# Cross-attention and expert feed-forward on one core: keys and queries as two float32r terms in two row tiles instead of three bf16 terms in one

## What is computed

```python
x = x + xattn(layernorm(x), ctx, ctx)     # x: (2, 512, 256); ctx: (2, 1024, 256); 16 heads of 16
#   q, k, v = heads(Q W_Q' + b_Q), heads(K W_K' + b_K), heads(V W_V' + b_V)
#   scores = einsum('bhqd,bhkd->bhqk', q, k) / 4 ; probs = softmax(scores) ; attn = probs v
#   return attn W_O' + b_O
x = x + ffn(layernorm(x))                 # shared expert (512 hidden, silu gate)
#   plus 8 routed experts (256 hidden, gelu), the two best per token, gates from sigmoid scores
```

## Time and the profile before

| | |
|---|---|
| median of 3 runs | 416.05 us (414.91 to 416.39) |
| the profiled execution | 414.85 us, its span 412.9 us |
| PE busy, share of span | 384.8 us, 93% |
| DVE busy | 308.0 us, 75% |
| ACT busy | 206.6 us, 50% |
| POOL busy | 138.7 us, 34% |
| mean granted TensorE clock | 0.988 |

### The profile page before, as it was taken

The page is one execution under the profiler, slowest core; times in us unless marked ns, Lnnn a source line. Parts: engine busy times, 40 slices in busy tenths (PEclk is TensorE's granted clock), DMA queues, the critical chain, the costliest instruction groups (busy, mean ns, idle before and its releaser), DMA issues.

```text
span 412.9 us, 6040 instructions
## 1 busy us (share of the span) xinstructions
PE 384.8 (93%) x2208; PEld 215.3 (52%) x2208; DVE 308.0 (75%) x487; ACT 206.6 (50%) x373; POOL 138.7 (34%) x147
## 2 busy tenths in 40 slices
PE   6775979999999999999999899999999979999996
PEld 2562557222222222227222224348898878899995
DVE  4498967988888879884888862505777986686885
ACT  4653433877776776763777967662133131412111
POOL 2649997000403104040040220101038757007750
PEclk9998989999999999999999989999999999999999
DMA  7678438006151240610610100001013222102331
GB/s 244 232 162 188 118 86 223 0 2 116 53 115 54 57 104 10 115 54 2 116 52 2 52 2 1 3 1 54 0 41 88 76 78 84 46 2 58 96 102 51
DMA packets 23964, 30.34 MB, mean 73 GB/s; under 512 B 4672, under 2 KB 20992, under 8 KB 23168
## 3 DMA queue, kind: packets, MB, share of 16 engines
q1 hardware_dynamic: 23936, 29.98, 28.4%
HBM read 24.00 MB, written 5.77 MB: 72 GB/s over the span
## 4 chain that ended last, share of the span: by engine, by line
PE 76%; DVE 11%; DMA 4%; ACT 3%; issue 3%; POOL 2%; SPq 1%; ACTq 0%; DVEq 0%
PE psum L933 32%; PE psum L1052 14%; PE psum L1017 14%; PE psum L1027 12%; DVE negm L826 6%; PE psum L1061 2%; ACT PB L618 2%; DMA PB<-in_ctxT_dram 2%; DVE x_sb L814 2%; POOL R L497 1%; DMA QS<-qs_d 1%; DMA qs_d<-RAW 1%; PE psum L945 1%; DVE WH L796 1%; DVE WH L797 1%
## 5 line engine op out<-in xcount | busy, mean ns | idle before, releaser
L826 DVE TENSOR_REDUCE negm<-psum 128x1 f32<-128x1024 f32 x128 | 150.9, 1218 | 27.6 <-PE psum L1027 26.6
L618 ACT ACTIVATE PB<-psum 128x512 f32<-128x512 f32 x256 | 133.4, 604 | 56.4 <-PE psum L1017 56.1
L1017 PE MATMUL psum<-QS,KS 98*128 98x512 bf16 x256 | 81.1, 384 | 3.6 <-ACT PB L618 3.3
L1027 PE MATMUL psum<-KS,QS 96*128 96x512 bf16 x256 | 78.0, 389 | 5.9 <-DMA QS<-qs_d 3.7
L633 ACT ACTIVATE PB<-psum 128x512 f32<-128x512 f32 x40 | 22.1, 596 | 93.4 <-PE psum L933 93.4
L1052 PE MATMUL psum<-PB,VA 128*17 128x512 f32 x512 | 68.0, 605 | 0.0
L556 POOL TENSOR_SCALAR R<-RAW 128x512 fp32r<-128x512 f32 x32 | 23.2, 725 | 120.1 <-DMA RAW<-in_ew_dram 62.7
L1017 PEld LDWEIGHTS psum<-QS,KS 98*128 98x128 bf16 x256 | 20.0, 96 | 77.1 <-ACT PB L618 57.3
L933 PE MATMUL psum<-R,WH 128*128 128x256 f32 (+1 forms) x336 | 51.9, 302 | 3.8 <-POOL R L497 2.9
L933 PEld LDWEIGHTS psum<-R,WH 128*128 128x128 f32 x336 | 45.9, 191 | 7.9 <-issue 5.0
L933 PE MATMUL psum<-XT,R 128*128 128x512 f32 x192 | 46.7, 392 | 0.0
(11 more groups left out here) (128 smaller groups left out, 388.0 us busy)
## 6 DMA issues: line engine op xcount, KB each, us to landing
RAW<-in_ew_dram SPq DMA_DIRECT2D x32, 256.0 KB, 2.7
ks_d<-PARTS SPq DMA_DIRECT2D x16, 192.0 KB, 2.8
KS<-ks_d SPq DMA_DIRECT2D x8, 384.0 KB, 4.7
QS<-qs_d SPq DMA_DIRECT2D x48, 64.0 KB, 4.9
KS<-ks_d SPq DMA_DIRECT2D x8, 256.0 KB, 5.4
qs_d<-RAW SPq DMA_DIRECT2D x8, 192.0 KB, 3.2
RAW<-in_sw_dram SPq DMA_DIRECT2D x6, 256.0 KB, 2.9
x_sb<-in_x_dram SPq DMA_DIRECT2D x2, 512.0 KB, 6.1
```

What stands on the lines that cost most here:

```text
L618: act.activation(PB[:, n % PR, i * N:(i + 1) * N], bank[(2 * n + i) % 3], ACT.Exp, scale=DK ** -0.5).then_inc(exp_done, 1)
L826: dve.tensor_reduce(negm[:, g % 2, r // QT, r % QT:r % QT + 1], psum[:, k0:k0 + 2, :].rearrange("p a n -> p (a n)"), AX.X, ALU.max, negate ...
L1017: pe.matmul(bank[t % 3], KS[s][0:KROWS + 2, j, k0:k0 + P], QS[s][0:KROWS + 2, j, :], start=True, stop=True).then_inc(scores_done, 1)
L1027: last = pe.matmul(ring_bank(st, half), QS[s][0:KROWS, j, qt * P:(qt + 1) * P], KS[s][0:KROWS, j, half * N:(half + 1) * N], start=True, st ...
```

## The change

Keys and queries become two float32r terms (hi, lo). The stack of a group has 48 rows, the three products hi x hi, hi x lo, lo x hi, and two bias rows. It lies twice in the partitions: KS rows 0 to 49 hold the first 512 keys, rows 64 to 113 the other 512; QS holds the same queries in both halves. A score pair is now the same 128-key offset in either half (rows 0 to 49 and 64 to 113), so that its two matmuls use different row tiles of 64 rows, and so do the two matmuls of a maximum. Per K or Q job ACT writes the high term, DVE the low one straight from PSUM (one `scalar_tensor_tensor`), and POOL nothing; a ring of six part buffers takes the place of three. Stores and loads of the stacks move 4 bytes an element. The transpose of the maxima is in float32. `xn` has a buffer of its own, and `nrow` one slot.

```diff
-TERMS = 6
+TERMS = 3
+HP = P // 2
-POOL_MID = 6
+PARTS_RING = 6
-        QS = [sb(f"QS{i}", [P, GH, S], BF16) for i in range(SLOTS)]
-        KS = [sb(f"KS{i}", [P, GH, T], BF16) for i in range(SLOTS)]
+        QS = [sb(f"QS{i}", [P, GH, S], F32R) for i in range(SLOTS)]
+        KS = [sb(f"KS{i}", [P, GH, T // 2], F32R) for i in range(SLOTS)]
...
+            def store_parts(c):
+                kind, b, m, tb = kq_jobs[c]
+                n = jobs.index(kq_jobs[c])
+                sp.wait_ge(job_free[n % 4], n // 4 + 1)
...
+                    if kind == "K":
+                        sp.dma_start(dst[:, 0, :], half[:, 0, :]).then_inc(kq_stored[c][l], 16)
+                        sp.dma_start(dst[:, 1:3, :], half).then_inc(kq_stored[c][l], 16)
...
             def load_stack(g):
+                if g < SLOTS:
+                    sp.wait_ge(ones, g + 1)
+                for tb in range(2):
+                    sp.wait_ge(stored_k[tb][l], 32)
+                    sp.dma_start(raw(KS[s][tb * HP:tb * HP + KROWS, :, :]),
+                                 ks_d[b, m, l, :, :, :, tb * N:(tb + 1) * N].rearrange("p d j t -> (p d) j t"))\
                         .then_inc(stk_loaded[s], 16)
+                sp.wait_ge(stored_q[l], 32)
+                for tb in range(2):
+                    sp.dma_start(raw(QS[s][tb * HP:tb * HP + KROWS, :, :]),
+                                 qs_d[b, m, l].rearrange("p d j t -> (p d) j t")).then_inc(stk_loaded[s], 16)
...
                 for c in range(2):
-                    sp.dma_start(QS[g % SLOTS][KROWS + c:KROWS + c + 1, :, :],
-                                 nrow[GH * c:GH * c + GH, g % 2, :]).then_inc(bias_loaded[g % 2], 16)
+                    for tb in range(2):
+                        r = tb * HP + KROWS + c
+                        sp.dma_start(raw(QS[g % SLOTS][r:r + 1, :, :]), nrow[GH * c:GH * c + GH, :])\
+                            .then_inc(bias_loaded[g % 2], 16)
...
-                    act.activation(TMP[:, c % 3, :], bank[n % 4][:, :], ACT.Identity, bias=bias).then_inc(kq_hi, 1)
-                    act.activation(parts[c % 3][:, 0, :], bank[n % 4][:, :], ACT.Identity, bias=bias)\
-                        .then_inc(job_free[n % 4], 1)
+                    act.activation(parts[c % PARTS_RING][:, 0, :], bank[n % 4][:, :], ACT.Identity,
+                                   bias=kq_bias(kind, m)).then_inc(kq_hi, 1)
...
-                if kind in "KQ" and kq_of[jobs[n]] < POOL_MID:
+                if kind in "KQ":
-                    link(dve.tensor_tensor(TMP[:, c % 3, :], TMP[:, c % 3, :], parts[c % 3][:, 0, :], ALU.subtract))
-                    dve.tensor_copy(parts[c % 3][:, 1, :], TMP[:, c % 3, :]).then_inc(kq_mid, 1)
+                    dve.scalar_tensor_tensor(out=lo, in0=bank[n % 4][:, :], scalar=kq_bias(kind, m), in1=raw(hi),
+                                             op0=ALU.add, op1=ALU.subtract).then_inc(job_free[n % 4], 1)
...
-                        k0 = (2 * kp + i) * P
-                        pe.matmul(bank[t % 3], KS[s][0:KROWS + 2, j, k0:k0 + P], QS[s][0:KROWS + 2, j, :],
+                        rows = slice(i * HP, i * HP + KROWS + 2)
+                        pe.matmul(bank[t % 3], KS[s][rows, j, kp * P:(kp + 1) * P], QS[s][rows, j, :],
...
-                        last = pe.matmul(ring_bank(st, half), QS[s][0:KROWS, j, qt * P:(qt + 1) * P],
-                                         KS[s][0:KROWS, j, half * N:(half + 1) * N], start=True, stop=True)
+                        rows = slice(half * HP, half * HP + KROWS)
+                        last = pe.matmul(ring_bank(st, half), QS[s][rows, j, qt * P:(qt + 1) * P],
+                                         KS[s][rows, j, :], start=True, stop=True)
...
-                                         nhl[:, g % 2, qt].rearrange("p c j -> p (c j)"), identb[:, :],
+                                         raw(nhl[:, g % 2, qt].rearrange("p c j -> p (c j)")), ident[:, :],
```

More of the change, by code:

```diff
@@ L136, in xattn_ffn @@
     steps += [("mid", 3), ("split", 4), ("mid", 4), ("stats", 1), ("job", 5), ("rstd", 1), ("job", 6), ("mid", 5)]
-    steps += [("norm1", 1), ("ones", 0), ("job", 7), ("split", 5), ("mid", 6), ("split", 6), ("mid", 7), ("ones", 1)]
+    steps += [("norm1", 1), ("job", 7), ("split", 5), ("mid", 6), ("split", 6), ("mid", 7), ("ones", 1)]
     m = 0
@@ L391, in _ @@
               .then_inc(ld_rows, 16)
-            term_rows = [(3, slice(0, 3 * DK)), (2, slice(3 * DK, 5 * DK)), (1, slice(5 * DK, 6 * DK))]
+            def store_parts(c):
+                kind, b, m, tb = kq_jobs[c]
+                n = jobs.index(kq_jobs[c])
+                sp.wait_ge(job_free[n % 4], n // 4 + 1)
+                src = raw(parts[c % PARTS_RING])
+                for l in range(2):
+                    half = src[l * HP:(l + 1) * HP]
+                    if kind == "K":
+                        dst = ks_d[b, m, l, :, :, :, tb * N:(tb + 1) * N].rearrange("p d j t -> (d j) p t")
+                        sp.dma_start(dst[:, 0, :], half[:, 0, :]).then_inc(kq_stored[c][l], 16)
+                        sp.dma_start(dst[:, 1:3, :], half).then_inc(kq_stored[c][l], 16)
+                    else:
+                        dst = qs_d[b, m, l].rearrange("p d j t -> (d j) p t")
+                        sp.dma_start(dst[:, 0:2, :], half).then_inc(kq_stored[c][l], 16)
+                        sp.dma_start(dst[:, 2, :], half[:, 0, :]).then_inc(kq_stored[c][l], 16)
@@ L411, in load_stack @@
-                sp.wait_ge(stored_q, 32)
-                for n, rows in term_rows:
-                    for r0 in range(rows.start, rows.stop, DK):
-                        sp.dma_start(QS[s][r0:r0 + DK, :, :].rearrange("r j t -> r (j t)"),
-                                     qs_d[b, hg // 2, hg % 2, 3 - n].rearrange("d j t -> d (j t)"))\
-                            .then_inc(stk_loaded[s], 16)
+                m, l = hg // 2, hg % 2
+                stored_k, stored_q = kq_stored[kq_count(b, m):][:2], kq_stored[kq_count(b, m) + 2]
@@ L737, in route @@
                 ts = slice(4 * b, 4 * b + 4)
-                (lg, e_, s_, sel_, eq, w_, oh, oh2, both, prod) = (rt[:, i, ts] for i in range(10))
+                (lg, e_, s_, sel_, eq, w_, oh, oh2, both, prod) = (rt[b][:, i] for i in range(10))
                 dst = comb[:, ts, :]
@@ L1051, in _ @@
                     for j in range(GH):
-                        last = pe.matmul(acc[32 * j:32 * j + DK + 1, :], VA[:, b, 2 * kp + kk, GH * hg + j, :],
+                        last = pe.matmul(acc[32 * j:32 * j + DK + 1, :], VA[:, b, kp + KP * kk, GH * hg + j, :],
                                          PB[:, (4 * q + j) % PR, kk * N:(kk + 1) * N],
```

112 lines of the change are left out of this document (34 added, 78 removed).

## The result

The changed kernel takes 445.72 us (median of 4 runs, 443.3 to 446.53), the kernel before beside it 415.48 (413.83 to 416.39): the ratio is 1.0723, interval 1.0667 to 1.0779. It is 30 us slower. The forecast was 415.3, in a range from 402 to 427: the prediction is wrong.

The account below looks back on a forecast made before the run. The closed loop score, exponential, fourth score, maximum, pv was taken to bound the kernel. Terms -6.4, +4.2, 0, +2.0, -1.0, 0, +0.5 sum to -0.7: 414.15, plus 1.2 for the median, 415.3 us; range 402 to 427.

Parts of the forecast that it names:

- The clock falls in the waits: Rival: TensorE's waits let its granted clock fall; judged small, as a period is still 87% busy; chance 0.02.
- The period: Two units in the loop: 2.75 us instead of 2.88, 49 periods, -6.4 us (-9.8 to -2.9).
- The reading of the loop: Score, exponential, fourth score, maximum, pv form a closed loop; the fourth score waits for ACT's first exponential, until 1.13 us.
- A float32r weight load adds some 0.02: Up to a period's fourth score: the load moves the end of the wait for ACT from 1.13 to 1.15 us.
- The transposes: Transposes of the maxima, between pv and the next score: float32 instead of bf16, +0.53 us, 8 times, +4.2 us.
- The front: Up to the first units: first maximum unchanged (-1.6 to +2.1), DVE's low terms +2.0 us, two `nhl` operations -1.0 us.
- The alternating tile sizes: V jobs and hidden-layer parts between 64-row matmuls: 13 places, tile changes against pair savings, about 0 (-2 to +2).
- The DMAs in the loop: Bias rows 0; `recip` up to 1 us late in five groups with a stack load; +0.5 us.
- DVE didn't become the limit: Rival: the fourth score doesn't hold the loop, whose stretch shrinks to DVE's time; 396 us, chance 0.12.
- The row tiles do not run side by side: Rival: a pair's matmuls follow one another; period 2.97 us, 428 us in all, chance 0.10.
- 2.9 or more, the tiles don't overlap: Sign in the timeline: a two-unit period of 2.9 us or more would mean the row tiles don't overlap.
- The doubled traffic: Rival: doubled store and load bytes put the first maximum at 37 us and delay `recip`; 422 us, chance 0.12.

Follow-up runs that it names:

- Run 6: The kernel before with only its score and maximum slices cut to 50 and 48 rows instead of 98 and 96, still bf16: 449.12 to 481.31 us.
- run 13: The changed kernel with scores over rows 0 to 113 and maxima over rows 0 to 111, full height, still float32r: 434.9 us, ratio 1.0471.
- run 3: The changed kernel with the row-sum DMAs of groups 0 to 5 issued on ACT's queue, not SP's: 446.45 us, ratio 1.0731.
- run 4: The changed kernel with the second score of each odd unit behind the maximum, for units 1 to 105: 439.38 us, ratio 1.0584.
- run 10: The kernel before, all bf16, with the second score of each odd unit behind the maximum: 411.86 us, ratio 0.9884.
- Run 8: The changed kernel with the transposes of the maxima in bf16 again: 433.2 us, ratio 1.0451.
- run 1: The changed kernel with each score matmul of units 0 to 5 and 106 to 127 issued twice: 441.54 us, ratio 1.0609.
- run 2: The changed kernel with short full-height float32 identity matmuls added at the scores of units 0 to 5 and 106 to 127: 474.94 us, ratio 1.1452.
- run 5: The changed kernel with both scores of a unit in the same 64-row tile, maxima keeping their two tiles: 460.63 us, ratio 1.11.
- run 7: The changed kernel with scores and maxima reading only the upper 16 bits as bf16, in the same row tiles: 426.97 us, ratio 1.0269.
- run 12: The changed kernel with bf16 transposes of the maxima, the second score behind the maximum, and repeated score matmuls together: 438.77 us, ratio 1.0522.
- run 11: The changed kernel with each job's two terms stored once and the doubled high term made by eight load DMAs a stack: 438.86 us, ratio 1.0542.
- run 9: The 66-row run: the kernel before with scores and maxima over 66 rows, in a tile of full height: 414.76 to 431.71 us.
- run 14: The changed kernel with a matmul over rows 0 to 113 added ahead of each score of units 0 to 5 and 106 to 127: 475.51 to 491.41 us.
- run 15: The changed kernel with only the maxima in full height, rows 0 to 111, scores keeping their row tiles: 455.12 us, ratio 1.0918.

## Why the prediction was wrong

**The step that failed** is the last rival, "The clock falls in the waits", with its reason "a period with 0.35 us of waiting is still 87% busy. Small", and a chance of 0.02. It was argued from how busy TensorE is. Run 6 has TensorE busy without a gap at 1.2 GHz, the fall at 272 us has no wait ahead of it, and run 13 brings the clock back with the same type, the same order and more rows: the number of rows at work makes the difference between the kernels, and not the waits. Of the 31.4 us, the rows give it this: the stretches at the lower level, 78 to 91, 251 to 262 and 271 to 293 us, are 46 us long, and with 1.58 of 4.47 lost in them it is 16 us. In the last one more is lost: from one pv to the next, with two products of the router between, it takes 6.03 us (273.68 to 279.71), where the kernel before took 3.24 (253.16 to 256.40); with that share the sum is 19. Run 13 gives another size: 11 us faster although some 49 periods are 0.24 us longer, so 23. The clock is some 16 to 23 of the 31 us, by these estimates. By the first, 4.6 of it lie ahead of the load behind group 0 (+8.9, of which +4.8 were there at the first unit) and 11.6 in the last region (+15.7). The kernel before falls too, for some 3 us at a time, at about 36, 59 and 238 us, and comes back. In the changed kernel the falls at two of these places of the program, 36 and 251 us there, last 14 and 10 us, and those at 77 and 272 us begin where the kernel before has none: half-height matmuls let the clock fall and keep it down. Yet in the loop, from 100 to 230 us, the same matmuls hold 2.4 GHz in this trace, and in those of runs 3 and 4 not all the way. How long a stretch lasts differs between executions: run 3's kernel is the changed one up to there, and its stretch at 77 us ends at 84 and not at 92.

**The period.** The reading of the loop was right: pairs side by side, the gain given to the wait, the fourth score the one that matters. Runs 4 and 10 confirm it: with the maximum put in the wait the period goes from 2.90 to 2.65, and from 2.88 to 2.82 in the kernel before. The size was wrong. "A float32r weight load adds some 0.02" was 0.12: the second matmul of a pair starts 0.11 us after the first, the exponential as much later, and the fourth score 1.25 us into the period instead of 1.13. From it to pv 0.67 us go by (103.45 to 104.12), where 0.61 was forecast, inside its bounds. The term -6.4 measured about +1. The bounds of 0.06 and 0.20 a period had left out nothing gained.

The Trainium skill (TensorE: Matmul & The Clock Gate, part 3, "The mechanism") says that a weight load overlaps a running matmul only where their row groups differ. I set this aside because 48 products of 256 columns over the same rows took 0.12 each, loads and all. The changed kernel shows 0.11 us within the first pair behind pv, whose two matmuls lie in different row groups, and nothing of it in the maximum's pair that follows (0.24 us for both). So the rule isn't what these rows show either, and neither it nor my extrapolation gives 2.90; the 2.97 worked out from it was nearer.

**The transposes.** Forecast +0.53 each, 8 times, +4.2. Measured 0.96 against 0.32, +0.64 each, +5.1. That it came so near is luck. The 0.85 us of the earlier trace rows are of the transposes of x at 36.80 us, where the clock is 0.50; four of them at 2.4 GHz start 0.11 us apart (38.84, the next T job), which is 0.44 in all. They are another form of the instruction besides, with one record each where the float32 products of `negmax` have two. The one error hid the other. Run 8 gives the 5 us back, and some 7 us besides.

**The front.** The first maximum was due between 33.3 and 37, taken as unchanged; it came at 38.35, +3.4, outside the bounds. The four loads of the stack took 12.6 us from the first issue (25.74) to the landing, the last one 10.04, where 7.9 had been worked out for all four. The assumed 200 GB/s were about right, 216 from 26 to 38.3 us, but that is 2.7 MB, and the stack is 1.57 of it. In the traces of runs 1 to 5, 7, 8 and 12 the first maximum comes at 36.06 to 37.70. It is at 37.37 or later in every trace, run 6 among them (37.46), where the clock is at 1.2 GHz for 3 to 7 us between 12 and 22 us, in jobs whose matmuls are the same in both kernels, and at 37.03 or earlier in all the others. So 1 to 2 of the 3.4 us seem to belong to the execution and not to the change. From there to the first unit DVE's added work was to give +1.0, and the first unit is at 75.06 instead of 70.25, +4.8 in all: +1.4. That this fits is in part luck. Three low terms ahead of the 16th maximum: 0.66 us each in the chain of waits, 2.0, as forecast. The two `nhl` operations of the first group take 0.39 us (62.58 to 62.97) instead of 1.69 (56.16 to 57.85), -1.3, where -1.0 was forecast. Not forecast: up to 51 us TensorE at 1.2 GHz, and not DVE, sets the pace (six products of a V job take 2.86 us at 44.66, where they took 1.38 at 49.54 before). The transposes of the first group take 1.03 us instead of 0.38, and the B job behind them 1.92 instead of 3.13, since the kernel before has its fall at 59 us just there.

**The alternating tile sizes** were to cost about 0. A maximum and the 12 products between two of them take 2.05 us ahead of the first unit (70.17 to 72.22), where they took 1.88 (65.71 to 67.59): +0.17 for one of five. In the last units, where the clock is up again, it is 3.64 us from pv to pv (295.00 to 298.64) instead of 3.48 (265.92 to 269.40): +0.08 for one of eight. If all are alike it is +1.5 us together, inside the bounds of 2.

**The DMAs in the loop.** `recip` was allowed to be 1 us late. It waits up to 2.04 us, 12.2 us of DVE's time in all, where 0.5 us had been put down. Of the +4.8 us of the four groups 2.6 are the transposes of four groups; the other 2.2 are the row sums and the period together, which no run parts. Run 3 takes 4.4 us of the waits away and gains nothing, so most of DVE's wait seems to be slack.

**The rivals.** DVE didn't become the limit: in the loop it is busy for 85.98 of 100 us. "The row tiles do not run side by side" was wrong as a mechanism (run 5, and the pair of 0.24 us), though "2.9 or more, the tiles don't overlap" would have read it so: the period is 2.90 for another reason. That rival was to decide from 0.33 us a pair on, which its own terms don't give: two pairs and a score at 0.236 reach the 1.13 us of the wait only at 0.45 a pair. The doubled traffic is right in kind: the first maximum is 1.1 to 3.4 us later than in the kernel before, by trace, and the row sums come late.

**What stays open.** Why the loop holds 2.4 GHz with matmuls of half height while the stretches ahead of it and behind it don't; what starts and what ends a stretch at the lower level; and how much of the gains of runs 1, 8 and 11 is a matter of where the falls happen to lie in an execution. The 66-row run shows that executions of one kernel can go either way. No run has float32r transposes or weight loads alone changed in a kernel whose clock stays up.

## What to carry to other kernels

Matmuls cut to fewer rows can leave TensorE at 1.2 GHz for ten or twenty us, however busy it is. Two of the four long stretches here began where the kernel before had a short dip of the granted clock, and two, the longest among them, where it had none: a clock of 0.988 in the kernel as it is doesn't promise that the one with fewer rows keeps it. So try the number of rows first, by itself, as run 6 does with two slices changed. Pairs of row tiles save time only if TensorE's issue holds the period; here the period was a loop through ACT, and moving one matmul into its wait (run 10) gave 1.2% where the rebuilt stacks lost 7.2%. Don't alternate tiles of two heights: in runs 14 and 15 it cost more than either height alone. And a price read from a row holds for the clock of that row: look at the granted clock beside it.

## What the runs showed of the hardware that was not expected

- TensorE busy for 20.00 of 20.00 us with 50-row bf16 matmuls, at a granted clock of 0.50 (run 6); 98 rows in the same windows are at 1.00.
- The changed kernel falls to 1.2 GHz at 272 us behind 4 us in which TensorE was busy for 4.00. 66 rows in bf16, in a tile of full height, have 0.50 at 80 to 90 us too, in one execution of 426.43 us (run 9).
- The scores of a unit in one row tile have a lower clock than in two: 0.907 (run 5) and 0.921.
- Two float32r matmuls in different row tiles start 0.11 us apart right behind pv, and the maximum's two, which follow, together: 0.24 us for the pair, as one matmul takes.
- A score of 50 rows between matmuls of 114 rows takes 0.72 us at 1.2 GHz, where a pair of 48 rows in two row tiles takes 0.43: 0.29 us for each change of height.
- A DMA of the row sums takes 4.6 us from issue to `recip` behind a stack load on its queue (108.75 to 113.31), and 4.95 us on another queue, with the stack load under way beside it.
